# Splitting queries and keys into three bf16 parts: from one engine to three

## The reference

```
x = x + 0.5 * ffn(layernorm(x))        # 8 routed experts (top 2) and a shared expert
x = x + attention(layernorm(x))
x = x + 0.5 * ffn(layernorm(x))        # the same weights as the first

attention:  q = n @ Wq + bq            # 16 heads of 8
            k, v = n @ Wk + bk, n @ Wv + bv     # 4 key and value heads
            p = softmax(q k^T / sqrt(8) + slope_h * (key - query), causal)
            out = (p v) @ Wo + bo
```

## Time and profile before

| | |
|---|---|
| time, median of 3 runs | 749.88 us (749.0 to 750.06) |
| the profiled execution's own time | 747.74 us |
| its span | 746.0 us |
| PE busy | 699.1 us, 94% |
| DVE busy | 582.6 us, 78% |
| ACT busy | 403.4 us, 54% |
| POOL busy | 112.5 us, 15% |

### The profile page before, as it was taken

One profiled execution on the slowest core, in us unless ns is written; L12 is line 12 of the kernel. 1 busy time (PEld: TensorE's weight loads), 2 busy tenths in 40 slices (PEclk: granted clock), 3 DMA queues, 4 the chain that ended last, 5 costly groups with the idle time before them and its releaser, 6 DMA issues.

```text
span 746.0 us, 15875 instructions
## 1 busy us (share of the span) xinstructions
PE 699.1 (94%) x5880; PEld 367.9 (49%) x5880; DVE 582.6 (78%) x1921; ACT 403.4 (54%) x579; POOL 112.5 (15%) x122
## 2 busy tenths in 40 slices
PE   4999998976999999999999999999999886999998
PEld 3554487842344444444444444444444274554498
DVE  5987458787999999999999999999999047766311
ACT  2353333132667777776777677777767832343300
POOL 2111962110000000000000000000000002102960
PEclk9999999975799999999999999999999997999999
DMA  7013633442110101001100101110010000005751
GB/s 215 0 17 67 107 57 97 143 151 77 31 39 25 28 26 39 20 20 38 36 23 20 39 21 29 29 37 21 20 38 1 2 1 0 2 0 89 104 95 57
DMA packets 47249, 34.69 MB, mean 47 GB/s; under 512 B 13106, under 2 KB 46514, under 8 KB 47172
## 3 DMA queue, kind: packets, MB, share of 16 engines
q1 hardware_dynamic: 46596, 33.60, 19.3%
q10 hardware_dynamic: 576, 0.08, 0.1%
HBM read 23.01 MB, written 10.39 MB: 45 GB/s over the span
## 4 chain that ended last, share of the span: by engine, by line
PE 53%; DVE 13%; issue 11%; ACT 2%; DVEq 0%; ACTq 0%
PE ps L1017 49%; DVE mx L902 8%; PE ps L1022 4%; DVE mx L895 1%; ACT h_all L623 1%; DVE h_all L895 1%; DVE xn L704 1%; DVE stats L692 0%; DVE wb L922 0%; DVE mm_ L919 0%; DVE sg L837 0%; ACT osb L612 0%; DVE idle L893 0%; DVEq L132 0%; DVE mv L696 0%
## 5 line engine op out<-in xcount | busy, mean ns | idle before, releaser
L623 ACT ACTIVATE h_all<-ps 128x1024 f32<-128x1024 f32 (+3 forms) x384 | 291.3, 811 | 112.1 <-PE ps L1017 108.9
L902 DVE TENSOR_REDUCE mx<-ps 128x1 f32<-128x512 f32 (+2 forms) x352 | 223.0, 681 | 9.2 <-PE ps L1017 6.7
L1017 PE MATMUL ps<-ks,xnT_all 57*128 57x512 bf16 (+3 forms) x768 | 179.1, 336 | 14.7 <-DVE mx L895 6.4
L1017 PE MATMUL ps<-h_all,vb 128*32 128x512 f32 (+3 forms) x1536 | 163.6, 499 | 0.6 <-ACT osb L612 0.6
L1017 PE MATMUL ps<-xnT_all,ks 59*128 59x512 bf16 (+3 forms) x768 | 158.9, 332 | 3.3 <-ACT h_all L623 3.1
L895 DVE CUSTOM_DVE_ANT_0 h_all<-ps,mask_w 128x384 bf16<-128x384 f32 (+1 forms) x256 | 149.3, 618 | 2.2 <-issue 0.5
L1017 PEld LDWEIGHTS ps<-ks,xnT_all 57*128 57x128 bf16 x768 | 56.4, 94 | 142.9 <-DVE mx L895 64.9
L1017 PE MATMUL ps<-cb 64*128 64x64 bf16 (+3 forms) x1216 | 112.9, 215 | 0.0
L716 DVE TENSOR_TENSOR h_all<-ps,sg 128x512 f32<-128x512 f32 x80 | 55.2, 690 | 55.5 <-PE ps L1017 53.8
L562 ACT ACTIVATE sg<-ps 128x512 f32<-128x512 f32 x80 | 47.8, 597 | 85.9 <-PE ps L1017 85.7
L1017 PEld LDWEIGHTS ps<-cb 64*128 64x128 bf16 x1216 | 80.1, 96 | 17.3 <-issue 1.0
(11 more groups left out here) (118 smaller groups left out, 539.5 us busy)
## 6 DMA issues: line engine op xcount, KB each, us to landing
xnT_all<-q_scr SPq DMA_DIRECT2D x64, 96.0 KB
attn<-sel_scr SPq DMA_DIRECT2D x12, 256.0 KB, 7.3
mask_second<-sel_scr SPq DMA_DIRECT2D x12, 256.0 KB, 8.3
q_scr<-qp SPq DMA_DIRECT2D x8, 384.0 KB
ks<-k_scr SPq DMA_DIRECT2D x64, 48.0 KB
x<-in_x SPq DMA_DIRECT2D x8, 256.0 KB, 6.1
yT<-sel_scr SPq DMA_DIRECT2D x8, 256.0 KB, 9.3
q_scr<-qp SPq DMA_DIRECT2D x8, 256.0 KB
```

The costliest lines, as they stand in the source:

```text
L623: act.activation(pr[:, (NSTEP * i + s) % PR_BUFS, p:HPG:SLOTS, lo:HALF], ps[:, b:b + 2, lo:HALF], ACT.Exp)\
L902: dve.tensor_reduce(m, src, AX.X, V.max).then_inc(a_out, 1)
L1017: return pe.matmul(o, l, r, start=start, stop=stop, skip_group_check=True)
```

## The change

`split` keeps its two subtractions on DVE (the rests) and loses its two casts and two second subtractions. The rests get a buffer with two halves (`qres` takes both halves of `sg`, `kres` is new). The second parts are now ACT copies, `second_parts(c-1)`, which stand behind `qk(c)` in ACT's list; those of group 7 stand behind the loop. The third parts are POOL subtractions, `third_parts(c-2)`, which stand behind `rsqrt(c)` in POOL's list; those of group 6 stand behind the loop, and those of group 7 behind `load_v(0, 0)`. Four semaphores are added: `qr`, `kr` (rests ready) and `qc`, `kc` (second parts ready). `qk(c)` now waits for the rests of group c-1, where it waited for its third parts, and a rest waits until the third parts of two groups before it were made. `pq` and `pk`, on which `store_parts` waits, are now set by POOL. The DVE chain of waits in `split` falls away.

```diff
--- before.py
+++ after.py
@@ -122,7 +122,7 @@
 
 FFN_SEMS = ("ve", "rs", "xn", "T", "xA", "gl", "lg", "sig", "sel", "mT", "mk", "md", "hm", "G", "U", "sg", "h", "tot", "tops",
             "wds", "Y", "x", "ch_up", "ch_down", "ve2", "rs2", "xn2", "Tb", "xTb", "Q", "K", "V", "qf",
-            "kf", "pq", "pk", "v", "dw0", "dw1", "out")
+            "kf", "qr", "kr", "qc", "kc", "pq", "pk", "v", "dw0", "dw1", "out")
 FfnSems = namedtuple("FfnSems", FFN_SEMS)
 
 
@@ -242,7 +242,8 @@
 
         qf = sb("qf", [P, GN])
         kf = sb("kf", [P, P])
-        qres, kres = sg[:, 0, :], sg[:, 1, 0:P]
+        qres = sg
+        kres = sb("kres", [P, 2, P])
         qp = sb("qp", [P, 2, 3, GN], BF16)
         kp = sb("kp", [P, 2, 3, P], BF16)
         v_all = sb("v_all", [P, UNITS, SEQ // P, DH])
@@ -497,10 +498,19 @@
             pool.wait_ge(f1.xn, GROUPS)
             for c in range(AHEAD):
                 mask_hidden(f1, 0, c)
+            def third_parts(c, par):
+                pool.wait_ge(f1.qc, c + 1)
+                pool.tensor_tensor(qp[:, par, 2, :], qres[:, par, :], qp[:, par, 1, :], ALU.subtract).then_inc(f1.pq, 1)
+                pool.wait_ge(f1.kc, c + 1)
+                pool.tensor_tensor(kp[:, par, 2, :], kres[:, par, :], kp[:, par, 1, :], ALU.subtract).then_inc(f1.pk, 1)
+
             for c in range(GROUPS):
                 rsqrt(c, c % 2, f1.ve2, f1.xn2, f1.rs2)
                 if AHEAD + c < GROUPS:
                     mask_hidden(f1, 0, AHEAD + c)
+                if c >= 2:
+                    third_parts(c - 2, c % 2)
+            third_parts(GROUPS - 2, 0)
 
             pool.wait_ge(s_late, 16 * len(late_loads))
             pool.wait_ge(f1.rs2, GROUPS)
@@ -526,6 +536,7 @@
 
             pool.wait_ge(f1.v, GROUPS)
             load_v(0, 0)
+            third_parts(GROUPS - 1, 1)
             over_units(values_and_bo)
             pool.wait_ge(o_bo, BO_PARTS)
             over_groups(lambda c, par, first, last: rsqrt(c, par, f2.ve, f2.xn, f2.rs))
@@ -588,23 +599,32 @@
                 def qk(c, par):
 
                     act.wait_ge(f.Q, c + 1)
-                    after(act, f.pq, c)
+                    after(act, f.qr, c)
 
                     after(act, f.dw1 if par else f.dw0, 8 * STORES * (c - par))
                     act.activation(qp[:, par, 0, :], bank(5), ACT.Identity, bias=bqs[:, 0:1], scale=QSCALE)
                     act.activation(qf[:, :], bank(5), ACT.Identity, bias=bqs[:, 0:1], scale=QSCALE)\
                        .then_inc(f.qf, 1)
                     act.wait_ge(f.K, c + 1)
-                    after(act, f.pk, c)
+                    after(act, f.kr, c)
                     act.activation(kp[:, par, 0, :], ps[:, 4, P:2 * P], ACT.Identity, bias=bk[:, 0:1])
                     act.activation(kf[:, :], ps[:, 4, P:2 * P], ACT.Identity, bias=bk[:, 0:1]).then_inc(f.kf, 1)
+
+                def second_parts(c, par):
+                    act.wait_ge(f.qr, c + 1)
+                    act.activation(qp[:, par, 1, :], qres[:, par, :], copy).then_inc(f.qc, 1)
+                    act.wait_ge(f.kr, c + 1)
+                    act.activation(kp[:, par, 1, :], kres[:, par, :], copy).then_inc(f.kc, 1)
 
                 def body(c, par, first, last):
                     xn_T(c, par)
                     qk(c, par)
+                    if not first:
+                        second_parts(c - 1, 1 - par)
 
                 if qkv:
                     over_groups(body)
+                    second_parts(GROUPS - 1, 1)
 
             def out_evac(i, j):
                 act.wait_ge(a_pv, NSTEP * i + (QT if j == 0 else NSTEP))
@@ -828,19 +848,16 @@
 
             def ffn_down(f, qkv):
                 ch = Chain(dve, f.ch_down)
-                LN_LINKS, SPLIT_LINKS = 2, 2
-                LINKS = LN_LINKS + SPLIT_LINKS
+                LN_LINKS = 2
 
                 def split(c, par):
 
                     dve.wait_ge(f.qf, c + 1)
-                    dve.tensor_tensor(qres, qf[:, :], qp[:, par, 0, :], V.subtract)
+                    after(dve, f.pq, c - 1)
+                    dve.tensor_tensor(qres[:, par, :], qf[:, :], qp[:, par, 0, :], V.subtract).then_inc(f.qr, 1)
                     dve.wait_ge(f.kf, c + 1)
-                    ch.link(dve.tensor_tensor(kres, kf[:, :], kp[:, par, 0, :], V.subtract))
-                    dve.tensor_copy(qp[:, par, 1, :], qres)
-                    ch.link(dve.tensor_copy(kp[:, par, 1, :], kres))
-                    dve.tensor_tensor(qp[:, par, 2, :], qres, qp[:, par, 1, :], V.subtract).then_inc(f.pq, 1)
-                    dve.tensor_tensor(kp[:, par, 2, :], kres, kp[:, par, 1, :], V.subtract).then_inc(f.pk, 1)
+                    after(dve, f.pk, c - 1)
+                    dve.tensor_tensor(kres[:, par, :], kf[:, :], kp[:, par, 0, :], V.subtract).then_inc(f.kr, 1)
 
                 def values(c, b, half):
 
@@ -856,7 +873,7 @@
                     y = bank(y_bank(qkv, par)).rearrange("p (t f) -> p t f", t=GT)
                     dve.tensor_tensor(xt(c), xt(c), y, V.add).then_inc(f.x, 1)
                     if qkv:
-                        ch.at(0 if first else LINKS * c - SPLIT_LINKS)
+                        ch.at(LN_LINKS * c)
                         dve.wait_ge(f.x, c + 1)
                         ln_stats(c, par, ch, f.ve2)
                         early_maxima(early(c, 0))
@@ -867,7 +884,6 @@
                         early_maxima(early(c, 1))
 
                 def last_split():
-                    ch.at(LINKS * GROUPS - SPLIT_LINKS)
                     split(GROUPS - 1, 1)
 
                 over_groups(body)
```

## The result

| | before | changed |
|---|---|---|
| time, median of 4 runs | 749.96 us (749.0 to 750.06) | 760.96 us (760.63 to 765.68) |
| ratio to before | | 1.0168, 95% interval 1.0138 to 1.0198 |
| span of the profiled execution | 746.0 us | 758.6 us |
| DVE busy | 582.6 us | 571.3 us |
| POOL busy | 112.5 us | 125.4 us |

The change made the kernel 11.0 us slower; 760.5 was forecast. All ratios here compare undisturbed executions; the profiled execution of one experiment, the kernel before with four buffers, was disturbed (970.34 us at a granted clock of 0.65, against 742.6 to 747.9 us in its other five), so that only the times of those five are used.

What follows compares the result with a forecast made beforehand. PE carries the chain, DVE paces the changed loop, and the stores have no slack. First score 10.5 us late: 747.74 + 10.5 = 758.2, plus 2.14 for the median, 760.4 us (predicted 760.5); range 755 to 767.

Steps and rivals of the forecast that it cites:

- What DVE gives up: DVE's splits: 1.41 us less each, 11.3 over 8 splits, at most 4.2 us of it on the path.
- The first stack: Group 0's store starts 5.3 us late; piece 0 at 134.2, PE's wait growing from 1.37 to 6.6 us.
- SP's list: SP's stores and 18 loads (8.71 us) ahead of store 2: qk(4) starts at 156.4, 6.5 us later.
- The loop that closes: qk(g+2) waits for store g, whose third parts wait for qk(g+1): 10.7 us per group, qk(7) 12.1 later.
- The end of the loop: After qk(7), DVE's reductions and SP's load_maxima delay the first score by 10.5 us, to 200.6.
- The sum: Whole kernel: 747.74 + 10.5 = 758.2 us profiled; with the runs' median 2.14 higher, 760.4 us.
- Rival 1: Faster, 745.7 us: later stores stay hidden and DVE's 4.2 us come through; chance 0.05.
- Rival 3: Slower by one delay, 751 to 755.2 us: first stack's 5.3 lost once, loop doesn't close; chance 0.12.
- rival 4: Longer, 765.5 to 770 us: each turn a microsecond more, or PE enters attention at clock 0.50; chance 0.12.
- Rival 2: No change, 749.9 us: stores hidden, but POOL and DVE block each other, giving back 4.3 us; chance 0.03.

Runs made afterwards that it cites:

- the kernel before with four buffers: The unchanged kernel with four instead of two buffers of parts, so qk waits for the store of four groups before: 745.45 us, ratio 0.9933.
- the no-lag kernel: Changed kernel with ACT's second parts right behind their own group's qk and POOL's third parts one round sooner: 744.16 us, ratio 0.9929 to the kernel before.
- A: The kernel before the change, rerun in each of three sets of experiments: medians 749.2, 750.1 and 749.4 us.
- B: The changed kernel, with second parts on ACT and third parts on POOL, both lagging: 760.96 us, ratio 1.0168 to the kernel before.
- no lag on ACT: Changed kernel with only ACT's second parts moved right behind their own group's qk; POOL's third parts stay late: 750.13 us, ratio 1.0011 to the kernel before.
- four buffers: Here the changed kernel with four instead of two buffers of parts, all lags kept: 749.39 us, ratio 1.0017 to the kernel before.
- closing it from group 2 on alone: Changed kernel with the lags taken out for groups 0 and 1 only: 756.61 us, ratio 1.0083 to the kernel before.
- B with four buffers: Changed kernel with four instead of two buffers of parts, all lags kept: 749.39 us, ratio 1.0017 to the kernel before.
- all together: Changed kernel without lags, with stores in three steps and four buffers of parts: 737.39 us, ratio 0.9854 to the kernel before.

## Why the prediction was right

*What DVE gives up.* 11.3 us of busy time, measured 11.3. That at most 4.2 reach the end was a little low: the table has 4.2 to 5.9 where no lag takes them away, though the interval of the no-lag kernel (3.5 to 7.0 us below A) still holds 4.2. In B nothing of them is seen: DVE waited 23.2 us for ACT.

*The first stack.* Store 0 was forecast 5.3 us late, at 123.15; it started at 123.63, in a trace whose `qk(1)` is 0.2 later. Piece 0: 134.2 forecast, 134.97 measured. The wait of PE went to 7.2 us, 6.6 forecast.

*SP's list.* `qk(4)`: 156.4 forecast, 157.61 measured. The 18 loads took 142.14 to 150.26, 8.1 us where 8.7 were put.

*The loop that closes.* Right in kind: opening it at either end, by ACT's place (no lag on ACT, 10.8 us) or by four buffers (11.6 us), removes most of the cost, and closing it from group 2 on alone brings the turns of 11.2 us back. Each turn was 0.4 to 0.6 longer than worked out. Two terms were put too small. The third key part took 0.43 us where I took 0.30 (a line through the two rows that bounded it, 0.24 at 64 columns and 1.13 at 512, gives 0.36), and landing took 2.0 to 2.4 (166.70 to 168.73; 188.85 to 191.23), where the one row that I read had 1.78. That row was of a wait by SP; the kernel before already had 2.36 where ACT was the one that waited, from the end of store 2 (147.58, SP's timeline) to `qk(4)` at 149.94:

```profile
147.08 0.50 SPq L389 DMA_DIRECT2D k_scr<-kp  x1
```

So `qk(7)` was 2.7 behind its forecast, 1.2 of it from `qk(4)`.

*The end of the loop.* 10.5 us were forecast for the first score and 12.6 measured, mostly those turns. Which of the two paths comes last was a draw: DVE's reductions and `load_maxima` both let PE go between 202.4 and 202.8 (its weight load waited 0.22 us for the latter). Here the prediction left something out when it dismissed the store of group 7, because nothing in the first unit waits for its data. That is so, but SP waits until it landed before it loads the next maxima, and PE waited for these, first unit, in its timeline:

```profile
211.30 0.39 PE L1033 MATMUL ps<-xnT_all,ks 59*128 59x512 bf16 x2 [0.85 <-DMA xnT_all<-wt]
```

The chain that ended last runs through this wait, and not through the first score at 202.76: from `load_maxima` at 200.15 on over the issue of store 7, its landing and the next maxima. PE's product of weights and values ahead of it came 12.1 us later than in the kernel before (209.06 against 196.95), the next one 13.2 (212.52 against 199.36); at the end of the span it is 12.6 again.

The profiled executions moved by 12.9 us (747.74 to 760.63), the medians by 11.0. The sum added 2.14 us, by which the profiled execution of before lay below its median; in B it was only 0.33. That made up for the 2 us by which the first score came later than forecast, so that 760.5 against 760.96 is nearer than its terms: luck.

*The rivals.* Rival 1 needed the stores to stay hidden; without the lag its time was reached and passed (744.2), although ACT still waited 8.0 us for stores there. Rival 3 is nearest to B with four buffers. Of rival 4, each turn was longer, but by 0.4 to 0.6 us and not by one. Its other condition, a granted clock of 0.50 at the start of attention, was met in both kernels, from 190 to 194 us in A and from 202.7 to 204.7 in B, the shorter of the two. Rival 2, POOL and DVE in each other's way, was not seen at its price: DVE's normalising never met the third parts in B, and kept its 1.11 us. DVE's subtractions met POOL once, in the last split, beside POOL's key part and copy, DVE's rows first:

```profile
194.89 0.80 DVE L857 TENSOR_TENSOR sg<-qf,qp 128x512 f32<-128x512 f32 x1
195.62 0.32 DVE L860 TENSOR_TENSOR kres<-kf,kp 128x128 f32<-128x128 f32 x1
```

```profile
195.09 0.70 POOL L529 COPY vb<-v_all 128x64 f32<-128x64 f32 x1
```

The subtractions took 0.80 and 0.32 us instead of 0.68 and 0.28, POOL's copy 0.70 instead of 0.24. That agrees in kind with what the Trainium skill (SBUF — State Buffer, "Who interferes with whom") says of a DVE instruction with two SBUF inputs beside a GpSimd instruction that reads SBUF. How long either is held up, these few rows don't tell. The kernel before had such a meeting too: in its last split the same subtraction took 0.86 us, from 181.07, beside an addition of POOL that began at 180.12 and took 1.26. So such a meeting is not new in B.

What stays open: how the 16.8 us of the lag split between first stack and loop. Taking out the first stack's lag first gives 4.4 for it and 12.4 for the loop; with the loop opened by four buffers the lag still costs 8.1. The two aren't independent, and the buffers also take away waits that A had of its own.

## What to carry to other kernels

Where work is taken off a busy engine, ask first who consumes it and how long that consumer's slack is: here the parts fed stores that were already waited for, and parts that came 5 us later cost 11, since the wait for a buffer closed a loop (parts, store, landing, next parts) that was longer than the pace of the group. The cure was not to undo the move, but to place the moved instructions right behind what they need, let each DMA wait only for what it carries, and give the loop more buffers; each of these by itself took 11.6 to 16.8 us off the changed kernel, and all together gave 1.5% over the kernel before.

## What the runs showed of the hardware that was not expected

POOL's subtraction of 128 columns took 0.43 us beside 1.16 for 512, so a quarter of the width cost 37% of the time. A store's landing, from the end of its last issue to the next instruction of the engine that waited, was no constant. In the kernel before it took 1.78 and 1.71 us where SP waited (stores 0 and 1) and 2.36 and 2.22 where ACT did (stores 2 and 3); in the changed one it took 2.0 to 2.4, whoever waited. For the store of group 0 it was 1.78 against 2.36, both with SP waiting and nothing issued behind it. Why was not tried.
